# A fused attention and mixture-of-experts block on one core: opening steps in another order, sigmoid by way of silu, halo and logit size on ScalarE, other orders in the steps without a Gram

## The chip, the core and the metric

The kernel runs on one core of a Trainium2 chip. Five engines work side by side, each through its own list of instructions, and meet at semaphores: TensorE (PE in the profile, its weight loads PEld), VectorE (DVE), ScalarE (ACT), GpSimd (POOL), and SyncE (SP), which here only issues DMAs. The metric is the device time of one execution in microseconds; lower is better.

## The reference, cut to what matters

`x` is 8 x 2048 tokens of 256 features, float32.

```python
x = x + attn(layernorm(x));  x = x + ffn(layernorm(x))
# attn: no softmax, one energy matrix per sequence
K, V, Q = x @ wk.T, x @ wv.T, x @ wq.T
energy = einsum('bnd,bne->bde', K, V)                 # 64 x 64 for each of 8 sequences
out = (Q @ energy) * sqrt(3/64) @ wo.T
# ffn
scores = sigmoid(x @ Wr)                              # 8 experts
_, idx = top_k(scores + router_bias, 2)
w = scores[idx];  w = w / (sum(w) + 1e-9);  cw = scatter(w, idx)
hid = silu(x @ Wg[e]) * (x @ Wu[e])                   # e = 0..3, 128 wide
routed = sum_e cw[e] * (hid @ Wd[e]) + (cw[4] + cw[6]) * x + cw[7] * relu(x)
shared = causal depthwise convolution of 4 taps + conv_b
return routed + shared
```

## The kernel before

The 16,384 tokens are 32 groups of 512, four groups to a sequence. A software pipeline of 40 steps works on several groups at once: in step n, group n - LAG[stage] is in that stage (line 34: load -1, norm L 0, Gram A 1, query Q 2, attention B 5, router R 6, experts C 7, output Y 8). Steps 0 to 6 are written out by hand as `head()` on each engine; steps 7 to 39 are `body(st)`. The order of each engine's work is the order of that code; there is no scheduler.

The energy matrix comes from the Gram matrix of the normalised tokens (`gram_halves`, accumulated over four groups in the PSUM bank `ps_gram`). Every fourth step (9, 13, ..., 33) is a chain step: `chain_gramT`, `chain_p1`, `chain_et`, `chain_f` turn a finished Gram into the matrix `f1`/`f2` that `attention` multiplies by the queries. Steps 7 to 32 have a Gram. Step 33 is the last chain step; in steps 34 to 38 `drain()` is true, and 34 to 36 of them still have attention.

Float32 products are made of three or two products of float32r halves: ScalarE copies a PSUM bank to a high half (`xnT_high`, `x2T_out`, `q_high`, `hid_high`), VectorE subtracts it from the bank for the low half (`xnT_low`, `x2T_low`, `q_low`, `hid_low`); for the last expert the subtraction is GpSimd's (`last_low`, L1332).

What happens to one group from attention on, within two steps: VectorE's `residual` adds the attention to the input (L1057) and takes statistics (`norm2_stats`); GpSimd makes scale and shift (`norm_factors`, the shift at L1311); ScalarE normalises four tiles (`norm2`, L840). TensorE transposes them in two halves (`x2_transpose`, L533, into `ps_sh`), multiplies by the router's weights (`router`, L543), and ScalarE copies the logits (`logits_copy`). The sigmoid is 1 / (1 + e^-x): GpSimd's `power` computes e^-x with a pow (L1368, `enx`) and adds one (L1372, `den`); VectorE's `route` takes the reciprocal, adds the bias, finds the two best, and normalises their weights into `cw` (L1115). `weights_transpose` (L606) brings `cw` into rows, ScalarE copies them, SyncE writes them to DRAM and spreads them over the partitions into `cwb`.

The experts, two matrices each (`gate_up(st, k)`, k = 0 to 7, banks k mod 3): ScalarE's silu into `gate` (L763), GpSimd's product with `cwb` (`gate_weight`, L1327), VectorE's product with the other matrix (`hidden`, L1011), the two halves, and `down(st, stage, e)` into `ps_y`. `down` of expert 3 falls in the next step. The convolution runs along the tokens: ScalarE's first tap (`conv_begin`), three on VectorE (`conv_tap`, L1029); three columns of the group before are copied first (`halo`, L1162). VectorE's `output` adds everything up.

## Time and profile before

| What | us |
|---|---|
| Median of 3 runs | 893.69 |
| Lowest and highest | 892.45, 894.4 |
| The profiled execution's own time | 893.6 |
| Its span, first to last instruction | 891.8 |
| TensorE busy | 855.9 |
| VectorE busy | 741.1 |
| ScalarE busy | 628.7 |
| GpSimd busy | 572.7 |

The span is 1.8 us shorter than the execution's own time. Times in the rows count from the span's start. In a timeline row stand start, duration, engine, line, operation, output and inputs by name, shapes and count; brackets at its end give the engine's idle time before it and who ended it. Several equal instructions in a row share one row, with an x and their number. The granted clock of TensorE is given as a share of its full speed, 2.4 GHz.

### The profile page before, as it was taken

Reading aid. Unit: us, or ns where it says so; the run is one execution under the profiler, and the core shown is the slowest. Engines: PE = TensorE matmul, PEld = TensorE weight load, DVE = VectorE, ACT = ScalarE, POOL = GpSimd, SP = SyncE. Lnnn points to the kernel's source line nnn. Section 1 sums busy time; section 2 is a strip of 40 time slices with the busy share of each in tenths; the row PEclk is TensorE's granted clock in tenths of the full one; section 3 lists DMA queues with packets and bytes.
Section 4 is the critical chain, followed back from the end, with each engine's and each line's share of the span. In section 5 each row is a group of like instructions: output and inputs, shape, how many; then the busy total and the mean of one; then the engine's idle time right before and its main releaser. Section 6 shows DMA issues by size and latency. Waiting matters only on the chain.

```text
span 891.8 us, 16729 instructions
## 1 busy us (share of the span) xinstructions
PE 855.9 (96%) x5437; PEld 754.3 (85%) x5437; DVE 741.1 (83%) x2056; ACT 628.7 (71%) x1238; POOL 572.7 (64%) x654
## 2 busy tenths in 40 slices
PE   5789999999999999999999999999999999999997
PEld 4668989898888888988889888888888898788876
DVE  5758889988888998888898888899888887767775
ACT  5676777777687777778677777777777775655643
POOL 3336776667676657667666767666576766556663
PEclk9989999999999999999999999999999999999999
DMA  9111434543334543343544343454424344433333
GB/s 286 57 52 47 137 121 142 143 117 99 95 119 142 144 142 68 114 129 120 143 143 114 101 115 99 143 144 142 119 72 119 101 114 119 111 104 100 106 91 84
DMA packets 79446, 103.86 MB, mean 116 GB/s; under 512 B 6528, under 2 KB 58880, under 8 KB 79360
## 3 DMA queue, kind: packets, MB, share of 16 engines
q1 hardware_dynamic: 74752, 86.02, 30.4%
q0 software_dynamic: 4608, 16.78, 10.0%
q8 instruction: 43, 0.70, 0.3%
q14 instruction: 43, 0.35, 0.1%
HBM read 68.96 MB, written 17.04 MB: 96 GB/s over the span
## 4 chain that ended last, share of the span: by engine, by line
PE 66%; DVE 13%; POOL 12%; issue 5%; ACT 4%; DMA 0%; POOLq 0%; ACTq 0%; DVEq 0%
PE ps_gu L406 9%; PE ps_gu L408 9%; PE ps_gu L407 9%; POOL enx L1368 7%; PE ps_y L406 5%; PE ps_y L408 5%; PE ps_y L407 5%; PE ps_sh L543 4%; PE ps_sh L533 3%; POOL gate L1327 3%; PE ps_sh L516 2%; DVE stats L1065 2%; DVE acc L1057 2%; ACT x L840 2%; PE ps_y L456 2%
## 5 line engine op out<-in xcount | busy, mean ns | idle before, releaser
L1327 POOL TENSOR_TENSOR gate<-gate,cwb 128x512 f32<-128x512 f32 x128 | 167.5, 1309 | 127.8 <-ACT gate L763 126.4
L406 PE MATMUL ps_gu<-x2T_hi,wgu_hi 128*128 128x512 f32 x512 | 212.2, 414 | 0.0
L408 PE MATMUL ps_gu<-x2T_hi,wgu_lo 128*128 128x512 f32 x512 | 203.0, 396 | 0.0
L407 PE MATMUL ps_gu<-x2T_lo,wgu_hi 128*128 128x512 f32 x512 | 202.2, 395 | 0.0
L1368 POOL TENSOR_TENSOR enx<-inv_e,logits 128x32 f32<-128x32 f32 x32 | 177.5, 5546 | 8.6 <-ACT logits L756 8.6
L406 PE MATMUL ps_y<-wd_hi,hid_hi 128*128 128x256 f32 x512 | 152.8, 299 | 4.0 <-DVE hid_lo L1018 3.1
L1029 DVE SCALAR_TENSOR_TENSOR conv<-x2T,conv_w,conv 128x512 f32<-128x512 f32 x192 | 146.4, 801 | 0.0
L408 PE MATMUL ps_y<-wd_hi,hid_lo 128*128 128x256 f32 x512 | 145.3, 284 | 0.0
L407 PE MATMUL ps_y<-wd_lo,hid_hi 128*128 128x256 f32 x512 | 144.2, 282 | 0.0
L1011 DVE TENSOR_TENSOR hid<-ps_gu,gate 128x512 f32<-128x512 f32 x128 | 86.0, 672 | 39.2 <-POOL gate L1327 38.1
L408 PEld LDWEIGHTS ps_gu<-x2T_hi,wgu_lo 128*128 128x128 f32 x512 | 96.9, 189 | 22.5
L406 PEld LDWEIGHTS ps_gu<-x2T_hi,wgu_hi 128*128 128x128 f32 x512 | 97.6, 191 | 19.2 <-DVE hid L1011 3.0
L407 PEld LDWEIGHTS ps_gu<-x2T_lo,wgu_hi 128*128 128x128 f32 x512 | 97.4, 190 | 13.4
L406 PEld LDWEIGHTS ps_y<-wd_hi,hid_hi 128*128 128x128 f32 x512 | 98.5, 192 | 6.7 <-DVE hid_lo L1018 4.3
L763 ACT ACTIVATE gate<-ps_gu 128x512 f32<-128x512 f32 x128 | 75.3, 588 | 40.6 <-PE ps_gu L408 39.0
L1018 DVE TENSOR_TENSOR hid_lo<-hid,hid_hi 128x512 fp32r<-128x512 f32 x96 | 68.8, 716 | 41.6 <-ACT hid_hi L756 41.6
L756 ACT ACTIVATE hid_hi<-hid 128x512 fp32r<-128x512 f32 x128 | 80.2, 626 | 32.1 <-DVE hid L1011 31.5
L407 PEld LDWEIGHTS ps_y<-wd_lo,hid_hi 128*128 128x128 f32 x512 | 97.4, 190 | 1.6
L1306 POOL TENSOR_TENSOR mv<-mv,eps_ln 128x4 f32<-128x4 f32 x64 | 13.5, 211 | 132.2 <-DVE mv L1068 112.8
L408 PEld LDWEIGHTS ps_y<-wd_hi,hid_lo 128*128 128x128 f32 x512 | 97.1, 190 | 0.0
L840 ACT ACTIVATE x<-acc,shift,rstd 128x256 f32<-128x256 f32 x128 | 66.5, 591 | 8.8 <-POOL shift L1311 8.2
L824 ACT ACTIVATE xn<-xa,shift,rstd 128x256 f32<-128x256 f32 x128 | 66.0, 589 | 8.2 <-POOL shift L1311 8.1
(115 smaller groups left out, 1934.3 us busy)
## 6 DMA issues: line engine op xcount, KB each, us to landing
cwb<-cw_rows SPq DMA_DIRECT2D x128, 256.0 KB, 4.0
xa<-in_x SPq DMA_DIRECT2D x32, 512.0 KB, 7.5
acc<-in_x SPq DMA_DIRECT2D x32, 512.0 KB, 6.7
acc<-x POOLq DMA_DIRECT2D x32, 512.0 KB, 4.6
out<-acc SPq DMA_DIRECT2D x64, 256.0 KB, 2.3
cwb<-in_wg SPq DMA_DIRECT2D x4, 128.0 KB, 4.0
cwb<-in_wu SPq DMA_DIRECT2D x4, 128.0 KB, 3.8
cwb<-in_wd SPq DMA_DIRECT2D x1, 512.0 KB, 4.5
```

Source lines behind the costliest of these rows:

```text
L406: nc.tensor.matmul(dst, a_hi, b_hi, start=start, stop=False, skip_group_check=True)
L407: nc.tensor.matmul(dst, a_hi, b_lo, start=False, stop=False, skip_group_check=True)
L408: return nc.tensor.matmul(dst, a_lo, b_hi, start=False, stop=stop, skip_group_check=True)
L756: return nc.scalar.activation(dst, src, ACT.Copy, scale=scale)
L763: nc.scalar.activation(gate[:, e % 2], ps_gu[GU_BANK[2 * e]][:, :], ACT.Silu)\
L824: nc.scalar.activation(xn[:, q, t], xa[:, q, t], ACT.Identity, bias=shift1[:, f, t:t + 1], scale=rstd1[:, f, t:t + 1]).then_inc(xn_ready, 1)
L840: nc.scalar.activation(x2[:, q, t], acc[:, st.slot("B", 4), t], ACT.Identity, bias=shift2[:, q, t:t + 1], scale=rstd2[:, q, t:t + 1]).then ...
L1011: v.tensor_tensor(hid[:, e % 2], ps_gu[GU_BANK[2 * e + 1]][:, :], gate[:, e % 2], ALU.mult)\
L1018: v.tensor_tensor(hid_lo[:, k], hid[:, k], hid_hi[:, k].bitcast(F32), ALU.subtract)\
L1029: v.scalar_tensor_tensor(conv[:, c], x2T[:, q, c, k:k + GT], conv_w[:, c, k:k + 1], conv[:, c], ALU.mult, ALU.add).then_inc(conv_ready, 1)
L1327: g.tensor_tensor(gate[:, e % 2], gate[:, e % 2], cwb[:, q, e], ALU.mult).then_inc(gatew_ready, 1)
L1368: g.tensor_tensor(enx[:, :], inv_e[:, :], logits[:, :], ALU.pow).then_inc(enx_ready, 1)
```

## The change

Four things are changed.

1. The sigmoid. `power` and its two tiles go from GpSimd. ScalarE takes the absolute value of the logits from PSUM (`size`), adds 2^-100 (`mag`, `score_size`) and computes silu(-mag) (`dip`, `score_dip`). VectorE multiplies by the reciprocal of mag, which gives -sigmoid(-|x|), adds 1 where the logit is positive, and takes the absolute value: five operations in front of the bias where there was one. The 1e-9 is a ninth column of `raw`, set once, and its addition (L1106) goes.
2. `halo` moves from VectorE to ScalarE.
3. The opening. The transposes of groups 0 to 4 go to the banks of `ps_y` and `ps_gu` in turn and no longer through `ps_sh`; the chain of the first sequence comes before the first query product's use of the other groups; the first attention is followed by transposes, Gram and query product of the next groups, and only later by the second attention. ScalarE starts with a silu of one element (`spark`), and the program's ScalarE list then has one table load (before: two, the second ahead of the first silu of step 7). In step 7 VectorE takes both `x2T_low` ahead of the convolution's taps.
4. The steps without a Gram. TensorE runs `down(st, "C", 2)` before `weights_transpose` in steps 34 to 36. VectorE runs `residual` and `norm2_stats` ahead of `hid_low(1)`, and `route` is cut in two: `hid_low(2)` stands between its halves in steps 34 to 37. ScalarE runs `hid_high(2)` and then `silu(3)` ahead of `conv_begin`. In step 37 VectorE's `hidden(2)` now stands ahead of the route (before, behind it).

The diff, cut to its core:

```diff
@@ TensorE
             def weights_transpose(st):
                 pe.wait_ge(cw_ready, st.before("R", 1, 1))
...
+            def head_transpose(n):
+                if n >= 2:
+                    pe.wait_ge(xnTlo_ready, (n - 1) * HC)
+                elif n == 1:
+                    pe.wait_ge(wqlo_out, 1)
+                pe.wait_ge(xn_ready, (n + 1) * TG)
+                for c in range(HC):
+                    xn_move(at("A", n, NG), c, head_bank[n][c])
             def head():
...
+                head_transpose(0)
                 pe.wait_ge(w_loaded, 16 * N_LOADS)
                 chain_gramT(b)
                 chain_p1(b)
                 chain_et(b)
+                q_project(at("Q", 0, NG))
                 pe.wait_ge(et_out, b.chains(2, 2))
                 chain_f(b)
+                attention(b, 0)
+                attention(b, 1)
+                head_transpose(1)
+                gram_matrix(at("A", 4, NG))
+                head_transpose(2)
                 q_project(at("Q", 1, NG))
...
                 x2_transpose(r, 0)
                 x2_transpose(r, 1)
+                gram_matrix(at("A", 5, NG))
                 router(r)
+                attention(at("B", 1, NG), 0)
+                attention(at("B", 1, NG), 1)
+                head_transpose(3)
                 q_project(at("Q", 2, NG))
...
                 if a_on:
                     gram_halves(st)
+                if b_on and drain:
+                    down(st, "C", 2)
                 if r_on:
                     weights_transpose(st)
@@ ScalarE
                 copy(logits[:, :], ps_sh[0][:, 0:TG * NE]).then_inc(logits_ready, 1)
+                nc.scalar.activation(size[:, :], ps_sh[0][:, 0:TG * NE], ACT.Abs).then_inc(logits_ready, 1)
...
+                nc.scalar.activation(mag[:, :], size[:, :], ACT.Identity, bias=least[:, :]).then_inc(mag_ready, 1)
+                nc.scalar.activation(dip[:, :], mag[:, :], ACT.Silu, scale=-1.0).then_inc(dip_ready, 1)
...
+                if c_on and st.drain():
+                    hid_high(st, 2)
+                    silu(st, 3)
                 if r_on:
                     conv_begin(st)
-                if c_on:
+                if c_on and not st.drain():
@@ VectorE
-                dve.wait_ge(den_ready, st.before("R", 1, 1))
-                done(v.reciprocal(flat(score[:, :, :]), den[:, :]))
+                dve.wait_ge(mag_ready, st.before("R", 1, 1))
+                done(v.reciprocal(rmag[:, :], mag[:, :]))
+                dve.wait_ge(dip_ready, st.before("R", 1, 1))
+                after()
+                done(v.tensor_tensor(minor[:, :], dip[:, :], rmag[:, :], ALU.mult))
+                after()
+                done(v.scalar_tensor_tensor(signed[:, :], logits[:, :], 0.0, minor[:, :], ALU.is_gt, ALU.add))
+                after()
+                done(v.scalar_tensor_tensor(flat(score[:, :, :]), signed[:, :], -1.0, signed[:, :], ALU.mult, ALU.max))
@@ GpSimd
-                if r_on:
-                    power(st)
```

VectorE in a step without a Gram, from the second `hidden` to the start of the route. Before (L1018 is `hid_low`, L1057 `residual`, L1065 to L1068 the statistics, L1088 the route's start):

```order
L1011 TENSOR_TENSOR hid<-ps_gu,gate 128x512
L1018 TENSOR_TENSOR hid_lo<-hid,hid_hi 128x512
L1057 TENSOR_TENSOR acc<-ps_sh,acc 128x512 x2
L1065 BN_STATS stats<-acc 128x6 x4
L1002 COPY tick<-ident 1x1
L1068 BN_AGGR mv<-stats 128x2 x4
L1011 TENSOR_TENSOR hid<-ps_gu,gate 128x512
L1088 RECIPROCAL score<-den 128x32
L1090 TENSOR_TENSOR biased<-score,bias 128x4x8
```

Now (L1062 is `hid_low`, L1101 `residual`, L1142 to L1157 the route's first half):

```order
L1055 TENSOR_TENSOR hid<-ps_gu,gate 128x512
L1101 TENSOR_TENSOR acc<-ps_sh,acc 128x512 x2
L1109 BN_STATS stats<-acc 128x6 x4
L1046 COPY tick<-ident 1x1
L1112 BN_AGGR mv<-stats 128x2 x4
L1062 TENSOR_TENSOR hid_lo<-hid,hid_hi 128x512
L1055 TENSOR_TENSOR hid<-ps_gu,gate 128x512
L1142 RECIPROCAL rmag<-mag 128x32
L1145 TENSOR_TENSOR minor<-dip,rmag 128x32
L1147 SCALAR_TENSOR_TENSOR signed<-logits,minor 128x32
L1149 SCALAR_TENSOR_TENSOR score<-signed 128x32
L1151 TENSOR_TENSOR biased<-score,bias 128x4x8
```

The residual and its statistics have moved ahead of the first `hid_low`, and the route has grown by three operations here.

TensorE at the end of such a step. Before, from the last product of `gate_up` 7 (L606 is `weights_transpose`):

```order
L408 MATMUL ps_gu<-x2T_hi,wgu_lo 128x512
L606 MATMUL ps_sh<-ident,cw 16x128
L406 MATMUL ps_y<-wd_hi,hid_hi 128x256
L407 MATMUL ps_y<-wd_lo,hid_hi 128x256
L408 MATMUL ps_y<-wd_hi,hid_lo 128x256
```

Now, from the last product of `down` 2 (L600 is `weights_transpose`), with `gate_up` 0 of the next step behind it:

```order
L410 MATMUL ps_y<-wd_hi,hid_hi 128x256
L411 MATMUL ps_y<-wd_lo,hid_hi 128x256
L412 MATMUL ps_y<-wd_hi,hid_lo 128x256
L600 MATMUL ps_sh<-ident,cw 16x128
L410 MATMUL ps_gu<-x2T_hi,wgu_hi 128x512
L411 MATMUL ps_gu<-x2T_lo,wgu_hi 128x512
L412 MATMUL ps_gu<-x2T_hi,wgu_lo 128x512
```

The transposed weights now stand behind the twelve products of `down` 2.

GpSimd in a step with a Gram. Before (L1327 is the gate's product, L1368 the pow):

```order
L1327 TENSOR_TENSOR gate<-gate,cwb 128x512 x2
L1368 TENSOR_TENSOR enx<-inv_e,logits 128x32
L1372 TENSOR_TENSOR den<-enx,one_e 128x32
L1327 TENSOR_TENSOR gate<-gate,cwb 128x512
L1306 TENSOR_TENSOR mv<-mv,eps_ln 128x4
L1307 TENSOR_TENSOR negm<-zero,mv 128x4
L1309 TENSOR_TENSOR rstd<-mv,half_neg 128x4
L1311 TENSOR_TENSOR shift<-negm,rstd 128x4
L1327 TENSOR_TENSOR gate<-gate,cwb 128x512
```

Now (L1387 is the gate's product):

```order
L1387 TENSOR_TENSOR gate<-gate,cwb 128x512 x3
L1366 TENSOR_TENSOR mv<-mv,eps_ln 128x4
L1367 TENSOR_TENSOR negm<-zero,mv 128x4
L1369 TENSOR_TENSOR rstd<-mv,half_neg 128x4
L1371 TENSOR_TENSOR shift<-negm,rstd 128x4
L1387 TENSOR_TENSOR gate<-gate,cwb 128x512
```

The pow and the addition are gone from between the second and the third gate.

VectorE in step 7. Before (L1122 is `x2T_low`, L1029 a tap, L1011 the first `hidden`):

```order
L1183 TENSOR_TENSOR xnT<-ps_sh,xnT 128x512 x2
L1172 COPY x2T<-x2T 128x2x3
L1029 SCALAR_TENSOR_TENSOR conv<-x2T,conv_w,conv 128x512 x2
L1046 BN_STATS stats<-xa 128x6 x4
L1002 COPY tick<-ident 1x1
L1049 BN_AGGR mv<-stats 128x2 x4
L1122 TENSOR_TENSOR x2T_lo<-ps_sh,x2T_hi 128x512
L1029 SCALAR_TENSOR_TENSOR conv<-x2T,conv_w,conv 128x512 x2
L1122 TENSOR_TENSOR x2T_lo<-ps_sh,x2T_hi 128x512
L1011 TENSOR_TENSOR hid<-ps_gu,gate 128x512
```

Now (L1186 is `x2T_low`, L1073 a tap, L1055 the first `hidden`):

```order
L1235 TENSOR_TENSOR xnT<-ps_sh,xnT 128x512 x2
L1186 TENSOR_TENSOR x2T_lo<-ps_sh,x2T_hi 128x512 x2
L1073 SCALAR_TENSOR_TENSOR conv<-x2T,conv_w,conv 128x512 x2
L1090 BN_STATS stats<-xa 128x6 x4
L1046 COPY tick<-ident 1x1
L1093 BN_AGGR mv<-stats 128x2 x4
L1073 SCALAR_TENSOR_TENSOR conv<-x2T,conv_w,conv 128x512 x2
L1055 TENSOR_TENSOR hid<-ps_gu,gate 128x512
```

Both low halves stand ahead of the taps, and the halo's copy is gone.

## Rows read from the trace of the kernel before

**Rows 1.** The page's first table: busy time, share of the span, instructions.
```profile
PE 855.9 (96%) x5437; PEld 754.3 (85%) x5437; DVE 741.1 (83%) x2056; ACT 628.7 (71%) x1238; POOL 572.7 (64%) x654
```

**Rows 2.** Busy time by stretch; last columns PEclk, DMA share, GB/s.
```profile
38.80:59.60 20.80, 17.73 (x84) 15.12 (x85) 10.53 (x41) 14.71 (x28) 7.93 (x10) 0.75 0.00 1
792.00:817.00 25.00, 23.37 (x137) 20.53 (x137) 17.61 (x52) 14.06 (x28) 15.16 (x16) 0.93 0.37 106
817.00:840.50 23.50, 21.86 (x137) 19.18 (x137) 17.62 (x52) 14.06 (x28) 15.16 (x16) 1.00 0.38 113
```

**Rows 3.** Timeline, TensorE: first transposes of x2, and what follows.
```profile
274.79 0.74 PE L533 MATMUL ps_sh<-ident,x 128*128 128x128 f32 x4
275.28 0.36 PE L406 MATMUL ps_y<-wd_hi,hid_hi 128*128 128x256 f32 x1
...
745.01 0.60 PE L533 MATMUL ps_sh<-ident,x 128*128 128x128 f32 x4
745.37 0.37 PE L406 MATMUL ps_y<-wd_hi,hid_hi 128*128 128x256 f32 x1
```

**Rows 4.** Timeline of one step with a Gram, other engines.
```profile
262.79 0.69 DVE L1011 TENSOR_TENSOR hid<-ps_gu,gate 128x512 f32<-128x512 f32 x1 [1.41 <-POOL gate L1327]
265.12 1.29 POOL L1327 TENSOR_TENSOR gate<-gate,cwb 128x512 f32<-128x512 f32 x1 [0.68 <-ACT gate L763]
265.41 1.05 DVE L1101 SCALAR_TENSOR_TENSOR raw<-marked,score 128x32 f32<-128x32 f32 x1
266.72 0.25 DVE L1106 TENSOR_SCALAR wsum_eps<-wsum 128x4 f32<-128x4 f32 x1
272.38 0.59 ACT L756 ACTIVATE xnT<-ps_sh 128x512 fp32r<-128x512 f32 x1
272.83 0.20 POOL L1311 TENSOR_TENSOR shift<-negm,rstd 128x4 f32<-128x4 f32 x1
273.07 2.08 ACT L840 ACTIVATE x<-acc,shift,rstd 128x256 f32<-128x256 f32 x4
```

**Rows 5.** Timeline of one step without a Gram, all engines.
```profile
815.25 1.29 DVE L1106 TENSOR_SCALAR wsum_eps<-wsum 128x4 f32<-128x4 f32 x1
817.05 0.28 PE L606 MATMUL ps_sh<-ident,cw 128*16 128x128 f32 x1 [1.35 <-DVE cw L1115]
817.54 2.06 ACT L840 ACTIVATE x<-acc,shift,rstd 128x256 f32<-128x256 f32 x4
817.63 0.39 PE L406 MATMUL ps_y<-wd_hi,hid_hi 128*128 128x256 f32 x1 [0.30 <-DVE hid_lo L1018]
820.20 1.30 POOL L1332 TENSOR_TENSOR hid_lo<-hid,hid_hi 128x512 fp32r<-128x512 f32 x1 [3.69 <-ACT hid_hi L756]
822.29 0.36 PE L406 MATMUL ps_y<-wd_hi,hid_hi 128*128 128x256 f32 x1
```

**Rows 6.** Timeline: a pow beside a VectorE subtraction, both in SBUF.
```profile
779.28 5.43 POOL L1368 TENSOR_TENSOR enx<-inv_e,logits 128x32 f32<-128x32 f32 x1
783.49 0.69 DVE L1018 TENSOR_TENSOR hid_lo<-hid,hid_hi 128x512 fp32r<-128x512 f32 x1 [1.38 <-ACT hid_hi L756]
```

**Rows 7.** Timeline, TensorE: the last steps.
```profile
862.02 0.28 PE L606 MATMUL ps_sh<-ident,cw 128*16 128x128 f32 x1 [0.30 <-DVE cw L1115]
863.98 0.39 PE L406 MATMUL ps_y<-wd_hi,hid_hi 128*128 128x256 f32 x1 [1.68 <-DVE hid_lo L1018]
883.97 0.38 PE L406 MATMUL ps_y<-wd_hi,hid_hi 128*128 128x256 f32 x1 [0.49 <-DVE hid_lo L1018]
```

**Rows 8.** Timeline: end of the opening and first full step.
```profile
59.63 0.27 PE L606 MATMUL ps_sh<-ident,cw 128*16 128x128 f32 x1
63.52 1.25 PE L533 MATMUL ps_sh<-ident,x 128*128 128x128 f32 x8 [1.82 <-DVE xnT L1183]
70.67 0.68 DVE L1011 TENSOR_TENSOR hid<-ps_gu,gate 128x512 f32<-128x512 f32 x1
72.76 0.42 PE L406 MATMUL ps_gu<-x2T_hi,wgu_hi 128*128 128x512 f32 x1
```

More of the change, by code:

```diff
@@ L744, in body @@
                     xn_transpose(st, 0)
-                if c_on:
+                if c_on and not (b_on and drain):
                     down(st, "C", 2)
@@ L1226, in body @@
                 c_on, y_on, r_on, b_on, m_on = st.on("C"), st.on("Y"), st.on("R"), st.on("B"), st.chain()
-                if r_on:
-                    halo(st)
                 if c_on:
+                    if not st.later("C", 1):
+                        x2T_low(st, 0)
+                        x2T_low(st, 1)
                     dve.wait_ge(halo_ready, st.before("C", 1, 1))
@@ L1233, in body @@
                     norm1_stats(st)
-                if r_on:
+                if r_on and st.later("C", 1):
                     x2T_low(st, 0)
@@ L1251, in body @@
                 drain = st.drain()
+                if b_on and drain:
+                    residual(st, 0)
+                    residual(st, 1)
+                    norm2_stats(st)
                 if c_on:
```

269 lines of the change are left out of this document (134 added, 135 removed).

## The prediction

> **What bounds the kernel now.** I read the table of busy times first: TensorE is busy for 855.9 of 891.8 us [rows 1], so GpSimd's 572.7 us, from which the change takes most, are no bound by themselves. Then I went through the span by stretch and through TensorE's timeline for each idle time and each instruction that takes longer than its like. That gives four places where TensorE loses time.
>
> First, the steps with a Gram. TensorE shows no idle time there, yet the first four transposes of x2 last 0.49 us until the next product begins, where the same four take 0.36 us at 745.01 [rows 3]. I measured this distance for each of the 24 steps between 116 and 720 us: it is always above 0.36, by 0.13 to 0.50 us, and the excess sums to 6.0 us. TensorE waits here, tile by tile, for ScalarE's `norm2`. ScalarE begins it at 273.07, when the shift of GpSimd is there (272.83 + 0.20); ScalarE itself could start some 0.5 us behind the start of its previous copy at 272.38, at 272.88 [rows 4].
>
> Second, the steps without a Gram: TensorE waits 1.35 us for `cw` and 0.30 us for `hid_lo`, three times alike [rows 5]. Third, the granted clock. In two stretches with the same 137 matmul records and the same waits, one has 0.93 of full speed and takes 25.0 us, the other 1.00 and 23.5 us; TensorE's busy time differs by 1.51 us [rows 2]. So a drop to the 1.2 GHz level behind such a wait costs 1.5 us. It came behind one of the three equal waits. Fourth, the opening: TensorE has a granted clock of 0.75 between 38.8 and 59.6 us [rows 2] and waits 1.82 us at 63.52 [rows 8].
>
> The profiled execution took 893.6 us, 1.8 more than its span; the median shown is 893.69, so sums against the one hold for the other.
>
> **Steps with a Gram.** The pow goes, 5.43 us each [rows 6], on an engine that TensorE does not wait for directly. What it frees is the second half of a chain: the third gate's product no longer stands behind it, so `hidden(2)`, which waited 1.41 us for it until 262.79 [rows 4], can start when TensorE has finished `gate_up` 5, by its timeline near 262.3: 0.5 us sooner. The route then gets three operations more, each like the 0.19 us of its small neighbours with some 0.03 between, 0.67 us, and loses L1106 with 0.25 us up to the next one at about 0.29. Net: 0.5 - 0.67 + 0.29, some 0.1 us sooner. But the 1.29 us product of the fourth gate runs from 265.12 to 266.41, and `raw`, which needs about 0.19 us, lasted 1.05 us until 266.46 [rows 4]: it was held up until the product ended. That product starts where TensorE and ScalarE put it, so `raw` ends at 266.46 again, and only the operation behind it is saved: 0.29 us for `cw`, `hid_lo`, the residual and the shift. The shift comes 0.29 us sooner, and then ScalarE's own 272.88 binds: 0.19 us gained. Capped by each step's excess, 24 steps give 4.3 us. Bounds: nothing, if ScalarE's four added small operations (0.2 us each, like its logits copy) hold `norm2` back; 6.0 us, if all excess goes. I take 4.3, since ScalarE waits between 255.5 and 256.4 where the new work stands.
>
> The Trainium skill has a rule on this (SBUF — State Buffer, "Who interferes with whom"): a VectorE instruction with two SBUF inputs contends with a GpSimd instruction that reads SBUF, and the one that comes second blocks until the first is done. For the gate's product the trace agrees (`raw`, 1.05 us). For the pow it does not: a subtraction of two SBUF tiles inside a pow of 5.43 us took 0.69 us [rows 6]. By the rule taking away the pow would free VectorE of blocks as well and the whole excess of 6.0 us would go, a sum of 882.1 us in place of the one below; by the rows it frees nothing there, and I go by them.
>
> **Steps 34 to 36.** Let T be the end of `gate_up` 7. Before, `cw` came at T + 1.35 (in the step shown T is 815.55, read off the timeline), the transposed weights at T + 1.5, and `down` of expert 3 in the next step began at 822.29, T + 6.74 [rows 5]. Now `down` 2 fills T to T + 1.42 (12 products of 0.118), and `weights_transpose` starts at T + 1.45. The residual ahead of `hid_low(1)` brings `cw` to about T + 0.6. TensorE's next 4.3 us of work would put `down` 3 at T + 4.8. But ScalarE's weights copy, `norm2` and `hid_high(3)` and GpSimd's `hid_lo` all hang on `weights_transpose`: `hid_lo` ended 4.45 us behind it (821.50 against 817.05) [rows 5]. That is T + 5.9 now. So the wait is not removed but moved, to 1.2 us ahead of `down` 3, and a step gains 6.74 - 5.97 = 0.77 us; three give 2.3 us. Bounds: 0 and the full 1.65 us a step. The drop of the clock in one of three waits, 1.5 us, comes less often behind waits of 1.2 us: I put two thirds of it, 1.0 us.
>
> **Steps 37 to 39.** Before, the route waited for the pow, and `hidden(2)` for the route; TensorE waited 0.30 and 1.68 us [rows 7], and the clock fell behind it (1.5 us). Now `hidden(2)` runs when `gate_up` 5 is done, and `down` 2 has its input with the transposed weights. The longer route, held up once by the fourth gate's product, puts these at T + 1.05 to 1.75 in place of T + 0.47. `down` 2 then starts 0.7 to 1.3 us sooner; with half of the clock's 1.5 us that is 1.7 us. In the last step `hid_high(2)` ahead of `silu(3)` takes away the 0.49 us wait at 883.97 [rows 7]: 0.5 us. Behind `weights_transpose` hang SyncE's DMAs that spread the weights. For group 31 the first gate's product of step 38 began 7.4 us behind 862.02, of which 0.8 us were ScalarE busy with another copy; 6.6 us behind T + 1.05 to 1.75 it still comes in time for `gate_up` 4, to within 0.2 us. In steps 34 to 36 the DMAs start where they did. Bounds for both terms: 0.4 and 3.3.
>
> **Opening and step 7.** I followed the new order through with the durations of the old one. The Gram of group 3 ends 1 us sooner (no transposes ahead). But the first query product needs the low half of group 0, which VectorE now makes behind the split of the weights, and it stands ahead of `chain_f`: the first attention comes 0.6 us later. From there TensorE has more to do in each wait, and `weights_transpose` comes at about 57.6 instead of 59.63 [rows 8], bound by VectorE's route behind the low halves of group 4. `x2_transpose` comes at 62.1 instead of 63.52. In step 7 VectorE now has both `x2T_low` ahead of its taps and cannot begin them early: from 63.7 it has 5.8 us of work and one block of 1.25 us by a gate's product up to the first `hidden`, 71.1 against 70.67 [rows 8]. TensorE, which was slowed by its clock before and came to `gate_up` 4 at 72.76 [rows 8], gets there at 71.9, but behind a wait of 4 us, after which I expect the low clock, 1.6 us. Net, near 0. Bounds: 2.2 us sooner if the clock stays up and no block falls there; 2 us later if it also falls in the chain of the first sequence, where TensorE waits twice for 2 us. The table load of 1.28 us that goes from step 7 lies beside this wait for VectorE. The halo on ScalarE (0.15 us) lies in its waits for TensorE.
>
> **The sum.** 893.6 - 4.3 - 2.3 - 1.0 - 1.7 - 0.5 - 0 = 883.8 us.
>
> **The rivals.** (1) The opening pays too: the clock stays up through it, 2 to 3 us more, 881.3. For it speaks that TensorE's work is closer together, against it the wait of 4 us in step 7. (2) ScalarE's chain holds `norm2`, so the steps with a Gram give nothing: 893.6 - 5.5 = 888.1. For it: ScalarE's start could be only 0.19 us sooner at best. (3) The drain's wait only moves: clock drops stay, and steps 34 to 39 give 1.5 us in all: 893.6 - 4.3 - 1.5 = 887.8. (4) Both (2) and (3): 892.1, within what can be told from no change. (5) Slower. Place: the route in each step with a Gram. Mechanism: it has more operations with all operands in SBUF (`minor`, `signed`, `score`), and a second one is held up by a gate's product, which costs up to 1.1 us as `raw` does. It decides from the point where the residual starts later than at 267.93, as now; there is no slack, since the transposes wait already. If it is 0.4 us late in 25 steps: + 10 us, less 5.5 of the drain, 898.1. Against it: the third gate's product, the one that could fall on it, now comes 2.5 us before the route.
>
> **How the numbers follow.** Forecast 0.42; (1) 0.16; (2) 0.14; (3) 0.12; (4) 0.07; (5) 0.09. A difference of 0.2%, 1.8 us, is about what a measurement can tell from none. Faster: the forecast, (1), (2) and (3), 0.84; same 0.07; slower 0.09. The range runs from 880.0, all bounds of the drain and the opening together with the 4.3, to 889.5, past (2) and (3).
>
> **What would show it.** Right: the four transposes of x2 at 0.36 to 0.42 us up to the next product in steps with a Gram; a wait of about 1.2 us for GpSimd's `hid_lo` ahead of `down` 3 in steps 35 to 37 and none for `cw` in 34 to 36; `hidden(2)` released by TensorE; a wait of some 4 us for `hid` in step 7. Wrong: steps with a Gram no shorter than 25.4 us, or a new wait for `x` ahead of the transposes; TensorE waiting in the opening more than before; a granted clock below 0.75 there.

## The result, and the profile after

The changed kernel takes 891.18 us (median of 20 runs, 888.78 to 894.38); the kernel before took 895.19 in the runs beside it (892.0 to 901.95). The ratio is 0.9951, 95% interval 0.9936 to 0.9967: faster by 4.4 us, where 9.8 us were forecast, and the time lies above the range (880.0 to 889.5). The profiled run has a span of 888.3 us, 3.5 less than the one before, so the two profiles show most of the difference.

The page's first table of the changed kernel, to be read against [rows 1]:

```profile
PE 849.0 (96%) x5437; PEld 754.3 (85%) x5437; DVE 752.1 (85%) x2088; ACT 643.2 (72%) x1366; POOL 415.6 (47%) x590
```

GpSimd has lost 157 us of work and TensorE, which sets the time, has only 6.9 us less busy time, with 3.4 us more idle time. Where these come from is seen when the span is cut at the transposed weights (L606 before, L600 after), one row for each stretch:

| stretch, from one set of transposed weights to another | before | after | difference | forecast |
|---|---|---|---|---|
| start to step 6 | 59.63 | 59.60 | 0.0 | -2.0 |
| step 7 | 26.23 | 30.05 | +3.8 | +2.0 |
| 25 steps, nearly all with a Gram (85.86 to 739.84; 89.65 to 739.33) | 653.98 | 649.68 | -4.3 | -4.3 |
| the rest, to TensorE's last product | 148.4 | 145.5 | -3.0 | -5.5 |

(The forecast put the opening and step 7 at 0 together; -2.0 is its transposed weights at 57.6.) So one term came out as worked, one that was put at 0 cost 3.8 us, and one is too small. In this table, and wherever a length of "step 7" is given, a step ends with its transposed weights.

**Steps with a Gram.** The timeline of the changed kernel in the step that answers to [rows 3, 4], 3.04 us later in the span by TensorE's transposes of x2 (3.05 by the fourth gate's product):

```profile
268.17 1.30 POOL L1387 TENSOR_TENSOR gate<-gate,cwb 128x512 f32<-128x512 f32 x1 [1.85 <-ACT gate L765]
268.76 0.75 DVE L1167 SCALAR_TENSOR_TENSOR raw<-marked,score 128x32 f32<-128x32 f32 x1
275.60 0.20 POOL L1371 TENSOR_TENSOR shift<-negm,rstd 128x4 f32<-128x4 f32 x1
275.89 2.07 ACT L842 ACTIVATE x<-acc,shift,rstd 128x256 f32<-128x256 f32 x4
277.83 0.60 PE L531 MATMUL ps_sh<-ident,x 128*128 128x128 f32 x4
278.19 0.36 PE L410 MATMUL ps_y<-wd_hi,hid_hi 128*128 128x256 f32 x1
```

`raw` ends at 269.51, less the 3.04 at 266.47, as before (266.46): the fourth gate's product still holds it. The shift comes at 272.56 (0.27 sooner), `norm2` at 272.85 (0.22 sooner), and the four transposes last 0.36 us up to the next product where they took 0.49. Seven steps in 25, six of them behind a chain, keep 0.52 to 0.70 us; the others are at 0.35 or 0.36.

**Step 7.** TensorE and VectorE from step 6 to `gate_up` 4, to be read against [rows 8]:

```profile
59.60 0.28 PE L600 MATMUL ps_sh<-ident,cw 128*16 128x128 f32 x1 [2.04 <-DVE cw L1179]
64.13 1.25 PE L531 MATMUL ps_sh<-ident,x 128*128 128x128 f32 x8 [1.82 <-DVE xnT L1235]
65.94 0.69 DVE L1186 TENSOR_TENSOR x2T_lo<-ps_sh,x2T_hi 128x512 fp32r<-128x512 f32 x1 [1.27 <-ACT x2T_hi L758]
67.53 2.50 DVE L1073 SCALAR_TENSOR_TENSOR conv<-x2T,conv_w,conv 128x512 f32<-128x512 f32 x2
73.03 0.67 DVE L1055 TENSOR_TENSOR hid<-ps_gu,gate 128x512 f32<-128x512 f32 x1
73.76 0.79 PE L410 MATMUL ps_gu<-x2T_hi,wgu_hi 128*128 128x512 f32 x1 [3.57 <-DVE hid L1055]
```

The wait of some 4 us is there (3.57), but all of it is 2 us later than worked out: the transposes of x2 at 64.13 and not 62.1, `hidden` at 73.03 and not 71.1, since TensorE waits 2.04 us for `cw` in step 6 (L600 at 59.60). The same stretch in the view by stretch, before first, then the changed kernel, then experiment e10 (below), in which no wait of step 7 is longer than 1.82 us. The last columns are PEclk (the granted clock), DMA share and GB/s:

```profile
59.60:85.80 26.20, 22.58 (x134) 19.48 (x133) 20.48 (x54) 18.07 (x34) 14.98 (x11) 0.93 0.26 76
```
```profile
59.60:89.60 30.00, 24.21 (x133) 20.58 (x134) 21.75 (x57) 17.45 (x37) 9.78 (x13) 0.89 0.25 67
```
```profile
57.80:82.00 24.20, 21.50 (x133) 18.27 (x134) 20.82 (x56) 18.57 (x39) 9.81 (x13) 1.00 0.29 80
```

TensorE's work takes 21.5 us at the 2.4 GHz level (e10, granted clock 1.00); the falls to the 1.2 GHz level cost 1.1 us before (22.58) and 2.7 us after (24.21), where the clock was 0.50 from 73.8 to 79.5, behind the wait of 3.57 us. The 3.8 us are then 2.2 of idle time (5.8 less 3.6) and 1.6 of clock.

**The last steps.** TensorE's waits in the changed kernel, against [rows 5, 7], and the pow of `norm2` of step 33 with what VectorE does beside it (the last two rows):

```profile
773.11 0.73 PE L531 MATMUL ps_sh<-ident,x 128*128 128x128 f32 x2 [2.15 <-ACT x L842]
816.16 0.28 PE L600 MATMUL ps_sh<-ident,cw 128*16 128x128 f32 x1 [0.21 <-DVE cw L1179]
820.63 0.39 PE L410 MATMUL ps_y<-wd_hi,hid_hi 128*128 128x256 f32 x1 [0.94 <-POOL hid_lo L1392]
861.51 0.28 PE L600 MATMUL ps_sh<-ident,cw 128*16 128x128 f32 x1 [1.87 <-DVE cw L1179]
872.15 1.09 PE L460 MATMUL ps_y<-ident,conv 128*128 128x128 f32 x8 [0.45 <-DVE conv L1073]
883.10 0.39 PE L410 MATMUL ps_y<-wd_hi,hid_hi 128*128 128x256 f32 x1 [1.41 <-POOL hid_lo L1392]
769.26 2.79 POOL L1369 TENSOR_TENSOR rstd<-mv,half_neg 128x4 f32<-128x4 f32 x1
769.75 1.39 DVE L1073 SCALAR_TENSOR_TENSOR conv<-x2T,conv_w,conv 128x512 f32<-128x512 f32 x2
```

The same place before:

```profile
769.46 0.67 DVE L1135 TENSOR_TENSOR q<-ps_gu,q 64x512 fp32r<-64x512 f32 x1
769.56 1.49 POOL L1309 TENSOR_TENSOR rstd<-mv,half_neg 128x4 f32<-128x4 f32 x1
770.07 0.73 DVE L1029 SCALAR_TENSOR_TENSOR conv<-x2T,conv_w,conv 128x512 f32<-128x512 f32 x1
770.08 0.06 DVE L1170 MEMSET x2T<- 128x6 f32 x1
770.73 0.73 DVE L1029 SCALAR_TENSOR_TENSOR conv<-x2T,conv_w,conv 128x512 f32<-128x512 f32 x1
```

From the transposed weights of step 33 TensorE is idle for 9.8 us before and 10.0 us after. The waits at the transposed weights of steps 34 to 36 and behind them are 1.14 us each in place of 1.64. But the stretch from the transposed weights of step 33 to those of step 34 (766.30 to 793.11 in the changed kernel; it is called step 33 from here on) has 2.8 us in place of 1.4, and the rest has 0.3 us more. What is gained here is granted clock: TensorE's busy time from 766 us on is 3.0 us shorter, 111.8 before and 108.8 after, with two drops before (0.93 in 792 to 817, 0.62 in 864 to 867) and none in this run of the changed kernel:

```profile
793.10:861.50 68.40, 63.33 (x391) 55.52 (x391) 54.59 (x146) 43.64 (x96) 27.15 (x38) 1.00 0.38 109
```

### The profile page after: what moved, and what is told of

Its sections match the earlier page's. It is cut to its first block, busy times and chain, and to the rows that moved or that the text cites. A ratio compares the mean times of both kernels' runs of the same rounds, so it can differ in the third digit from the quotient of the medians.

```text
span 888.3 us, 16852 instructions
## 1 busy us (share of the span) xinstructions
PE 849.0 (96%) x5437; PEld 754.3 (85%) x5437; DVE 752.1 (85%) x2088; ACT 643.2 (72%) x1366; POOL 415.6 (47%) x590
## 4 chain that ended last, share of the span: by engine, by line
PE 77%; DVE 9%; ACT 4%; issue 4%; POOL 4%; DMA 1%; POOLq 0%; DVEq 0%; ACTq 0%
PE ps_gu L410 11%; PE ps_gu L412 10%; PE ps_gu L411 10%; PE ps_sh L541 6%; PE ps_y L410 5%; PE ps_y L411 5%; PE ps_y L412 5%; PE ps_sh L531 3%; PE ps_y L460 3%; PE ps_sh L484 2%; POOL rstd L1369 1%; PE ps_gram L476 1%; PE ps_gu L564 1%; PE ps_sh L588 1%; PE ps_gram L618 1%
## 5 line engine op out<-in xcount | busy, mean ns | idle before, releaser
L1387 POOL TENSOR_TENSOR gate<-gate,cwb 128x512 f32<-128x512 f32 x128 | 165.7, 1294 | 277.4 <-ACT gate L765 269.3
L1073 DVE SCALAR_TENSOR_TENSOR conv<-x2T,conv_w,conv 128x512 f32<-128x512 f32 x192 | 153.6, 838 | 0.0
L1062 DVE TENSOR_TENSOR hid_lo<-hid,hid_hi 128x512 fp32r<-128x512 f32 x96 | 83.2, 866 | 38.1 <-ACT hid_hi L758 38.1
L1055 DVE TENSOR_TENSOR hid<-ps_gu,gate 128x512 f32<-128x512 f32 x128 | 86.2, 673 | 20.0 <-issue 13.4
L1366 POOL TENSOR_TENSOR mv<-mv,eps_ln 128x4 f32<-128x4 f32 x64 | 24.9, 388 | 136.6 <-DVE mv L1112 114.6
L1369 POOL TENSOR_TENSOR rstd<-mv,half_neg 128x4 f32<-128x4 f32 x64 | 67.2, 1050 | 5.0
```

The lines of the kernel that those rows point to most:

```text
L1055: v.tensor_tensor(hid[:, e % 2], ps_gu[GU_BANK[2 * e + 1]][:, :], gate[:, e % 2], ALU.mult)\
L1062: v.tensor_tensor(hid_lo[:, k], hid[:, k], hid_hi[:, k].bitcast(F32), ALU.subtract)\
L1073: v.scalar_tensor_tensor(conv[:, c], x2T[:, q, c, k:k + GT], conv_w[:, c, k:k + 1], conv[:, c], ALU.mult, ALU.add).then_inc(conv_ready, 1)
L1369: g.tensor_tensor(rstd, mv[:, :, 1], half_neg[:, :], ALU.pow).then_inc(rstd_ready, 1)
L1387: g.tensor_tensor(gate[:, e % 2], gate[:, e % 2], cwb[:, q, e], ALU.mult).then_inc(gatew_ready, 1)
```

## The experiments

Each is compared with the kernel before on the same chip; "span" is that of its one profiled run. Runs of one kernel differ by 1 to 10 us in this program (the kernel before: 892.0 to 901.95). Much of that goes with the clock: of the 11 runs of the kernel before that stand beside e9, the slowest, 901.13 us, has a mean granted clock of 0.979 and the fastest, 891.49, one of 0.992. So a mechanism is read in the trace from the stretch it sits in, and its worth from the ratio.

### e1: the opening of before in the changed kernel

All four `head()` functions and the waits and banks that go with them are as before; `spark`, `score_size`, `score_dip` and `halo` stay on ScalarE. In VectorE's `body`, step 7 has the order of before; the edit's first lines:

```diff
-                    if not st.later("C", 1):
-                        x2T_low(st, 0)
-                        x2T_low(st, 1)
...
```


> The changed kernel with the opening of the kernel before (all engines, with its banks and its order of VectorE in step 7; halo on ScalarE and the sigmoid from silu stay). Theory: the new opening and step 7 alone lose 3.8 us (the transposed weights of step 7, 89.65 against 85.86), and the Gram steps (-4.1) and the last steps (-3.0) keep theirs: span 884.5, some 3.8 us under the changed kernel, the transposed weights of step 7 at about 85.9. Rival: the gain of the Gram steps was there only because the changed opening leaves the engines in another phase; then those steps take 25.3 to 25.4 us each again and the span is about 888.

Measured: 889.56 us, ratio 0.9951 (0.9937 to 0.9966), span 887.3. Step 7 takes 26.19 us, as before (26.23), and the Gram steps keep their gain (649.8 us). But the transposed weights of step 6 came at 61.70 and not near 59.6, since the clock fell in the first chain (before, it was 1.00 in the same 8 us); the span missed the 884.5 expected by 2.8 us, 2.1 of them here:

```profile
30.00:38.00 8.00, 7.29 (x29) 5.76 (x28) 6.53 (x21) 4.27 (x10) 3.05 (x8) 0.57 0.00 1
```

So the rival is out, and the theory holds for step 7. The ratio is that of the changed kernel: what the new opening with its step 7 costs in the profile can't be told from such a drop (2 us), which comes in either order (0.50 in the changed kernel's 30 to 38 us).

### e2: the first taps of a step without Q behind the pow

```diff
+                    if not st.on("Q"):
+                        dve.wait_ge(rstd2_ready, st.before("B"))
                     conv_tap(st, 0)
```


> The changed kernel, with VectorE's first taps of each step that has no Q waiting for the pow of norm2 of the step before. Theory: the pow that takes 2.79 us at 769.26 (1.03 elsewhere) is held up by the two taps that VectorE runs beside it from 769.75 to 771.14; with the taps behind it, it takes 1.03 us, norm2 begins 1.7 us sooner, TensorE's wait of 2.15 us ahead of the transposes of x2 shrinks to about 0.4, and the span is 886.6. Rival: the pow is long for another reason (its operands, the DMA beside it): still near 2.8 us, TensorE waits as before or longer by the taps, 888.3 to 889.

Measured: 890.59 us, ratio 0.9966 (0.9954 to 0.9978), span 889.3. Step 33 takes 25.05 us in place of 26.81, and the pow is as short as elsewhere:

```profile
771.34 1.03 POOL L1371 TENSOR_TENSOR rstd<-mv,half_neg 128x4 f32<-128x4 f32 x1
773.43 0.73 PE L531 MATMUL ps_sh<-ident,x 128*128 128x128 f32 x2 [0.41 <-ACT x L842]
```

The theory holds to 0.1 us. The span, 886.6 expected, hides it: in this run the transposed weights of step 7 came 2 us later than in the changed kernel's (91.63), and the clock fell behind the wait of 1.87 us in step 37. The ratio shows no gain over the changed kernel's 0.9951.

### e3: another order on VectorE in step 7

```diff
+                seven = c_on and not st.later("C", 1)
                 if c_on:
-                    if not st.later("C", 1):
-                        x2T_low(st, 0)
-                        x2T_low(st, 1)
                     dve.wait_ge(halo_ready, st.before("C", 1, 1))
                     conv_tap(st, 0)
-                if st.on("L"):
+                    if seven:
+                        x2T_low(st, 0)
+                        x2T_low(st, 1)
+                if st.on("L") and not seven:
                     norm1_stats(st)
...
                     hidden(st, 1)
+                if seven:
+                    norm1_stats(st)
```


> The changed kernel, in step 7 alone with another order on VectorE: first taps, both low halves of x2, second taps, hidden 0, and the norm1 statistics (1.9 us) only behind hidden 1. Theory: TensorE's wait of 3.57 us for hidden 0 at 73.76 and the low clock behind it (to 79.5) come from the order on VectorE: hidden 0 starts at about 70 instead of 73.03, the wait shrinks to under 1 us, the clock stays up, the transposed weights of step 7 come at 84 to 86 instead of 89.65, span 882.5 to 885. Rival: VectorE has as much to do in step 7 either way, so the wait moves to the next product that needs a later hidden, and the statistics come late for norm1: at most 1 us gained, 887.5.

Measured: 889.95 us, ratio 0.996 (0.9946 to 0.9975), span 884.4, the transposed weights of step 7 at 85.53 (expected 84 to 86; 89.65 in the changed kernel):

```profile
64.41 2.45 DVE L1073 SCALAR_TENSOR_TENSOR conv<-x2T,conv_w,conv 128x512 f32<-128x512 f32 x2
66.78 1.27 DVE L1186 TENSOR_TENSOR x2T_lo<-ps_sh,x2T_hi 128x512 fp32r<-128x512 f32 x2
69.78 0.68 DVE L1055 TENSOR_TENSOR hid<-ps_gu,gate 128x512 f32<-128x512 f32 x1
67.61 2.22 PE L541 MATMUL ps_sh<-wr_sb,x2T 128*128 128x8 f32 x16 [1.00 <-DVE x2T_lo L1186]
```

The taps fill the time in which VectorE waited for ScalarE, `hidden` starts at 69.78, and of the wait of 3.57 us a wait of 1.00 us for the router is left. The clock fell all the same (0.52 in 69.7 to 72.6). The profiled run was the fastest of seven (886.21, their median 889.95), so the span flatters the edit: its ratio is no better than the changed kernel's.

### e4: VectorE's split of the weights later

```diff
-                split_weights()
...
                 f_low(b)
+                split_weights(0, 1)
...
                 xnT_low_head(1, 1)
+                split_weights(1, 2)
```


> The changed kernel, in the opening with VectorE's three low halves of the weights (3.5 us) behind the transposes of group 0 and the first F, in place of ahead of them. Theory: TensorE's wait of 2.10 us ahead of the first query product (29.31) goes, and with it the granted clock of 0.50 that holds from there to 38.7; the first attention begins at about 31 instead of 33.83, transposed weights of step 6 at 57 or sooner instead of 59.60, span some 2 us shorter, 886. Rival: the clock falls at the other waits of the first chain (0.37 us twice, 1.33 us) whatever the order, and what is gained is lost again at the wait for route: no gain, 888.3.

Measured: 890.86 us, ratio 0.9955 (0.9935 to 0.9975), span 890.0. The first chain ran at full clock, but the transposed weights of step 6 came at 59.91: TensorE waited 1.86 us for `norm2` at 40.63 and the route was no sooner. Of the rival, the first half fell (the clock stayed up) and the second holds: the gain is lost again ahead of the route, which hangs on something else.

```profile
30.00:38.00 8.00, 6.08 (x43) 5.53 (x43) 7.11 (x17) 6.36 (x14) 2.98 (x8) 1.00 0.01 2
```

### e5: the old order of step 7 alone

```diff
-                    if not st.later("C", 1):
-                        x2T_low(st, 0)
-                        x2T_low(st, 1)
...
-                if r_on and st.later("C", 1):
+                if r_on:
                     x2T_low(st, 0)
```


> The changed kernel, with VectorE's order in step 7 as before (first taps, norm1 statistics, low half 0 of x2, second taps, low half 1, hidden 0); the opening stays new. Theory: of the 3.8 us lost up to the transposed weights of step 7, most come from this order, which keeps VectorE idle until 65.94 and hidden 0 back to 73.03. With the old order hidden 0 comes at about 71.5 and TensorE's idle time is split in two (ahead of the router and ahead of gate_up 4), the step from 59.6 takes 26 to 27.5 us instead of 30.05: span 885 to 886. Rival: the loss comes from the opening steps (route and transposes of x2 in step 7 later by 0.6 us), the step takes 29 us or more: 887.5 to 888.3.

Measured: 892.31 us, ratio 0.9953 (0.9934 to 0.9973), span 890.8. The step takes 29.34 us: my expectation of 26 to 27.5 was wrong and the rival right. The taps come first, but a gate's product of GpSimd (64.83 to 66.36) falls on them and they last 2.45 us where they took 1.41 before, so the router waits 2.76 us for the low half:

```profile
64.46 2.45 DVE L1073 SCALAR_TENSOR_TENSOR conv<-x2T,conv_w,conv 128x512 f32<-128x512 f32 x2
64.83 1.53 POOL L1384 TENSOR_TENSOR gate<-gate,cwb 128x512 f32<-128x512 f32 x1 [4.54 <-DMA cwb<-cw_rows]
```

With the old opening ahead of it (e1) the old order took 26.19 us.

### e6: the old orders in the steps without a Gram

```diff
-                if b_on and drain:
-                    down(st, "C", 2)
                 if r_on:
                     weights_transpose(st)
...
-                if c_on and st.drain():
-                    hid_high(st, 2)
-                    silu(st, 3)
```

VectorE's order is `hid_low` 1, residual, `norm2_stats`, `hidden` 2, the route in one piece, `hid_low` 2 (in step 37 the route ahead of `hidden` 2), as before.

> The changed kernel with the orders of the kernel before in the steps without a Gram (TensorE's down 2 behind the transposed weights; VectorE's residual behind hid_low 1 and the route in one piece; ScalarE's hid_high 2 behind silu 3). Theory: TensorE's idle time in steps 33 to 39 is 10.0 us in the changed kernel and 9.8 in the one before, so the new orders moved waits and took none away; what the profile after has less (3.0 us) are two drops of the granted clock. Then the old orders give the same span but for drops: from the transposed weights of step 32 to the end 149.0 (no drop) to 152.0 us (two drops), time within 0.2% of the changed kernel or up to 1.5 us slower. Rival: the new orders are worth the idle time of steps 34 to 36 (0.5 us each) and more: 2.5 us slower in every execution.

Measured: 896.36 us, ratio 1.0001 (0.998 to 1.0021), span 893.7: the new orders are worth as much as the whole change, whose gain is gone without them, though the 25 steps keep theirs (649.8 us). My theory, that these orders were worth nothing, falls. TensorE waits 2.92 us in each of steps 34 to 36, not 1.64 as before:

```profile
816.08 1.27 POOL L1380 TENSOR_TENSOR gate<-gate,cwb 128x512 f32<-128x512 f32 x1
816.11 1.25 DVE L1152 COPY two<-top 128x8 f32<-128x8 f32 x1
819.08 0.28 PE L600 MATMUL ps_sh<-ident,cw 128*16 128x128 f32 x1 [2.62 <-DVE cw L1174]
```

The route, longer by three operations (four stand ahead of the bias where one stood, not five as the description of the change has it), stands behind the residual; one of its operations is held for 1.25 us by the fourth gate's product (before it was `wsum_eps`, 1.29 us [rows 5]), and more of the route comes after it. From step 33 on TensorE is idle for 13.7 us, 3.7 more than with the new orders; the pow of step 33 takes 2.79 us here too.

### e7: one small operation put back into the route

```diff
-                done(v.reciprocal(winv[:, :], wsum[:, :]))
+                done(v.tensor_scalar(wsum_eps[:, :], wsum[:, :], 0.0, None, ALU.add))
+                after()
+                done(v.reciprocal(winv[:, :], wsum_eps[:, :]))
```


> The changed kernel with one more small operation on VectorE in the route, behind the sum of the weights (where the kernel before added its epsilon; here it adds 0). Theory: in the Gram steps the end of the fourth gate's product sets raw, and what stands behind raw sets the shift: cw comes 0.25 to 0.29 us later, the first transposes of x2 last 0.49 to 0.58 us again in three of four steps, these 24 steps give back nearly all of their 4.1 us: span 892. Rival: the gain of these steps comes from the pow's absence (hidden 2 no longer waits, no contention), then they keep at least 3 of the 4.1 us: span 888 to 889.

Measured: 897.52 us, ratio 1.0013 (0.9996 to 1.003), span 891.5 (the profiled run, 893.3, was the fastest of twelve). The 25 steps take 654.2 us, 4.6 more than in the changed kernel and 0.3 more than before; the first transposes of x2 are at 0.50 to 0.64 us in most, at 0.85 or 0.86 behind a chain. In the step of [rows 4]:

```profile
269.11 0.25 DVE L1173 TENSOR_SCALAR wsum_eps<-wsum 128x4 f32<-128x4 f32 x1
277.11 0.82 PE L532 MATMUL ps_sh<-ident,x 128*128 128x128 f32 x4
277.69 0.36 PE L411 MATMUL ps_y<-wd_hi,hid_hi 128*128 128x256 f32 x1
```

The theory holds: the gain of the Gram steps hangs on one operation of 0.25 us behind `raw`. That the pow is gone (5.43 us) and the route has three operations more ahead of `raw` leaves nothing there to see; no run has the one without the other, so what each is worth alone is not shown.

### e8: e2 and e3 together

The edits are those two, unchanged.

> The two edits together that each shortened its stretch: VectorE's order in step 7 (first taps, low halves, second taps, hidden 0, statistics behind hidden 1) and its first taps behind the pow of norm2 in the steps with no Q. Theory: they are independent (3.95 us in step 7, 1.76 us in step 33): span 882.6, time some 4 to 6 us under the changed kernel on the same chip, if the clock falls as often. Rival: less idle time in one place brings the drop of the clock to another, as it seems for each edit alone (medians only 0.6 and 1.2 us under the changed kernel): within 2 us of it.

Measured: 885.97 us (883.5 to 888.96), ratio 0.9885 (0.9858 to 0.9912), span 884.4. Step 33 takes 25.06 us; step 7 takes 28.32 with only 2.4 us of idle time in it, since the clock was at 0.50 from 65.2 to 75.4 us of this run. Together they are worth more than the two ratios alone (0.9966, 0.996) let one expect; why is not shown.

### e9: last steps, `hid_high` 3 ahead of `norm2`; VectorE makes the last low half

```diff
                 if st.on("B") and st.drain():
+                    hid_high(st, 3)
                     norm2(st)
...
-                if c_on:
+                if c_on and not (st.on("B") and st.drain()):
                     hid_high(st, 3)
...
                     hidden(st, 3)
+                    if st.before("C") == NG - 1:
+                        hid_low(st, 3)
...
-                if c_on:
+                if c_on and st.before("C") != NG - 1:
                     last_low(st)
```


> The fastest kernel so far (step 7's order on VectorE and the taps behind the pow), with two edits in the last steps: where there is no Gram, ScalarE makes hid_high 3 ahead of norm2 instead of behind it, and in the last step VectorE (0.69 us) makes the low half of expert 3's hidden instead of GpSimd (1.26 us). Theory: TensorE's wait of 0.93 us for hid_lo ahead of down 3 comes from the 2.07 us of norm2 in front of hid_high 3; in its place at most 0.3 us for x are left, three times; the last wait of 1.41 us becomes 0.84. From the transposed weights of step 33 to the end 2.2 to 2.6 us less idle time than 8.3 us. Rival: norm2, now 0.5 us later, holds up the transposes of x2, and the wait only changes its name: under 0.8 us gained.

Measured on e8: 881.72 us (879.89 to 885.42), ratio 0.9854 (0.9819 to 0.9888), span 879.2. From step 33 on 5.0 us of idle time, where e8 has 8.3: more than expected, because no wait for `x` takes the place of the one removed.

```profile
810.31 0.63 ACT L758 ACTIVATE hid_hi<-hid 128x512 fp32r<-128x512 f32 x1
810.84 2.06 ACT L842 ACTIVATE x<-acc,shift,rstd 128x256 f32<-128x256 f32 x4
873.99 0.39 PE L410 MATMUL ps_y<-wd_hi,hid_hi 128*128 128x256 f32 x1 [0.80 <-DVE hid_lo L1063]
```

### e10: opening, the copies of group 4 ahead of `norm1` of group 6

```diff
-                norm1(at("L", 6, NG))
                 xnT_head(4, 0)
                 xnT_head(4, 1)
+                norm1(at("L", 6, NG))
```


> The fastest kernel so far, with one edit in the opening: ScalarE copies the transposes of group 4 ahead of norm1 of group 6 (2.08 us), not behind it. Theory: TensorE's wait of 2.04 us for the weights of group 0 ahead of the transposed weights of step 6 comes from the route, which stands on VectorE behind the low halves of group 4, and these behind ScalarE's copies; the route starts 1.2 us sooner (then VectorE's own work ahead of it binds), the wait shrinks to about 0.85 us and the transposed weights of step 6 come at 57.9 in place of 59.09. Rival: the third query product or norm2 of group 1 comes late instead, and the transposed weights stay at 59 or later.

Measured on e8: 881.62 us (880.89 to 881.89), ratio 0.9849 (0.9817 to 0.988), span 879.1. In the changed kernel (first two rows) and in e10 (the others):

```profile
52.12 2.08 ACT L826 ACTIVATE xn<-xa,shift,rstd 128x256 f32<-128x256 f32 x4
54.10 1.06 ACT L758 ACTIVATE xnT<-ps_y 128x512 fp32r<-128x512 f32 x2
```
```profile
51.55 1.09 ACT L758 ACTIVATE xnT<-ps_y 128x512 fp32r<-128x512 f32 x2
52.52 2.07 ACT L826 ACTIVATE xn<-xa,shift,rstd 128x256 f32<-128x256 f32 x4
57.77 0.28 PE L600 MATMUL ps_sh<-ident,cw 128*16 128x128 f32 x1 [0.75 <-DVE cw L1179]
68.82 0.50 PE L410 MATMUL ps_gu<-x2T_hi,wgu_hi 128*128 128x512 f32 x1 [0.47 <-DVE hid L1055]
```

The transposed weights of step 6 come at 57.77, where e8, which differs in this block alone, has them at 59.09 with the same wait of 2.04 us as the changed kernel. The first chain ran at a clock of 0.51 here too (30 to 38 us): this block, and not the clock, made the route 1.3 us late.

### e11 and e12: both edits, and the later split on top

e11 has the edits of e9 and e10, e12 that of e4 as well.

> Both of these edits on the fastest kernel so far. Theory: they add up, 3.4 to 3.8 us less than the 884.4 us of its profiled run: span about 881, time about 8 us less than the changed kernel. Rival: drops of the clock (1.5 us each, at different waits in each run) hide it: no more than 1.5 us under the fastest so far.

> The same with VectorE's low halves of the weights (3.5 us) taken behind the transposes of group 0, as tried before on the changed kernel. Theory: there it took the wait of 2.10 us ahead of the first query product away and the first chain ran at full clock, but the gain was lost again at the wait for norm2 (1.86 us at 40.63) and at the route; with norm1 of group 6 out of ScalarE's way the route is no longer late, and the transposed weights of step 6 come at 56 to 57. Rival: what ScalarE does between 34 and 40 us binds the opening whatever stands around it: no sooner than without this edit.

Measured: e11 879.9 us (878.64 to 880.76), ratio 0.983 (0.9795 to 0.9865), span 877.0; e12 878.83 us (876.4 to 881.39), ratio 0.9817 (0.9782 to 0.9851), span 878.1. e11's span is 7.4 us under e8's, but not as the sum of the two edits: step 7 is 3.8 us shorter, since the clock did not fall there in this run (24.5 us at 1.00), the last steps 3.8 us, and the opening is 0.3 us longer. The wait for `cw` in step 6 is 0.75 us as in e10, yet the transposed weights come at 59.41, for the whole opening of this run is 1.6 us later than e10's (the query product ahead of the experts at 54.74, there 53.10). By the medians e11 is 1.7 to 1.8 us below e9 and e10, and the three intervals overlap. In e12 the transposed weights of step 6 come at 57.40, sooner than e10's but not at 56 to 57, and the clock was at the 1.2 GHz level from 62.9 to 73.0 us of step 7; whether the later split is worth anything is open, the intervals overlap. Either beats both kernels clearly: 1.2 to 1.3% under the changed kernel, by its ratio of 0.9951.

## Why the prediction was wrong, and where it was right

**Steps with a Gram, -4.3 forecast, -4.3 measured: right by its mechanism, its size in part by luck.** The product holds `raw` (266.46 and 266.47), only the operation behind it is saved (0.27 against 0.29), `norm2` moves by 0.22 (0.19). e7 undoes it with that one operation. The rival that ScalarE holds `norm2` (2) and the slower one (5) are both out. The trace also bears out that the pow did not hinder VectorE here, against what the Trainium skill would give (SBUF — State Buffer, "Who interferes with whom"): the 6.0 us by the rule did not come. The even share was wrong, though. I capped every step's gain at 0.19 us; the six steps behind a chain gained nothing (25.43 us before and 25.46 after at the last of them), and the other steps from step 9 on gained 0.11 to 0.57 us each. The sum of the two errors is near zero.

**Opening and step 7, 0 forecast, +3.8 measured: the term that failed most.** Its step that `weights_transpose` comes at about 57.6, "bound by VectorE's route behind the low halves of group 4", is where it broke: it came at 59.60, behind a wait of 2.04 us for `cw`. I took VectorE's own queue as the bound and left out that these low halves need ScalarE's copies, which stand behind a `norm1` of 2.08 us; the route, now behind the low halves, inherits that. e10 moves this one block: against e8 the wait shrinks from 2.04 to 0.75 us and the transposed weights come 1.3 us sooner, at 57.77. The other half microsecond is not this block: the query product ahead of the experts came at 53.65 in the changed kernel's run and at 53.10 and 53.13 in e10's and e8's. The step for `hidden` in step 7 had the right work (5.8 us and a block of 1.25; measured 7.09 from 65.94 to 73.03) but started it 2.2 us too soon, at 63.7; from there its own terms give 70.75 and not the 71.1 of the text. The low clock, forecast at 1.6 us behind the wait, cost 2.7 in the whole step. The price I named as the bound for this (2 us later "if it also falls in the chain") was met in size by another cause: the clock did fall in that chain (0.50 in 30 to 38 us), but so it did in e10, and e4, where it did not, came to 59.91. It was also one of the signs named for being wrong, with TensorE waiting more in the opening: in the first 59.6 us it is busy for 40.55 us, before for 42.07.

**Steps 33 to 39, -5.5 forecast, -3.0 measured.** Four terms. (a) Steps 34 to 36: the wait for `cw` did move to `hid_lo` ahead of `down` 3 (0.94, forecast 1.2), but 0.21 us for `cw` stays, and a step has 0.50 us less idle time, not 0.77: -1.5 in place of -2.3. (b) Steps 37 to 39: nothing. The waits of 0.30 us for `cw` and 1.68 us for `hid_lo` became one of 1.87 us for `cw`, above the 1.05 to 1.75 forecast for the longer route; the 0.49 us at the end went into the 0.93 behind it (1.41), and 0.45 for the taps was new: +0.3 in all, in place of -1.45 (the two terms without their 0.75 of clock). (c) Step 33, which the prediction did not look at: +1.4, of which 1.1 is the wait behind the pow that the taps hold up (2.15 us, before 1.06) and 0.3 a wait for the residual ahead of the transposed weights of step 33. The pow takes 2.79 us in place of 1.49. e2 puts the taps behind it and has 1.03; so the taps hold it. Why they hold it for 1.3 us longer than before is not shown: in both kernels they start 0.5 us behind it and run back to back. What is gone from VectorE just there is the halo's MEMSET ahead of the taps, now on ScalarE, and every kernel of this document with the halo on ScalarE and no gate for the taps has the 2.79 us (e1, e3 to e7), but no run moves the halo alone. (d) The clock gave 3.0 and not 1.75, in these two profiles; over runs it cannot be told from these medians. And the terms did not stand alone: by e6 the longer route with the old orders waits 2.92 us in each of steps 34 to 36 where 1.64 stood before, 3.8 us in all, and the new orders first have to win that back. I had counted the new operations in the Gram steps and left them out in steps 34 to 36.

The lower end of the range, 880.0, was said to be all bounds of the drain and the opening with the 4.3 us. By the bounds as named (4.95 and 3.3 us for the drain, 2.2 for the opening, 1.0 of clock) it would be about 877.9. The result lies at the other end, so nothing hangs on it.

What stays open: what decides behind which wait the clock falls. The same wait of 1.82 us for the transposes of x2 in step 7 passed without a fall in e10 and with one in e8 (from 65.2 us on), and the 1.87 us for `cw` in step 37 without one in the changed kernel and with one in e2 (863.1 to 866.4).

## What to carry to other kernels

When an instruction is moved on one engine, follow its inputs on the others to the instruction that stands in front of them in the new order: a block of 2 us on ScalarE set a route on VectorE that looked bound by VectorE. A big operation taken off an engine that is not waited for need not show in the time: here the steps with a Gram gained by one operation of 0.25 us behind the one that is held, 4.3 us over 25 steps. What replaces it must be priced again in each kind of step. And in a kernel whose clock falls behind waits, it can pay to take the waits away in several places before judging by the time: two edits that alone had ratios (0.9966 and 0.996) no better than the changed kernel's 0.9951 had 0.9885 together.

## What the runs showed of the hardware

A GpSimd pow on 128x4 elements takes 1.01 to 1.04 us in 63 of the changed kernel's 64, and 2.79 us in the one that VectorE's taps run beside; with the taps behind it, 1.03. It had begun 0.49 us ahead of them, so here it was the first of the two that was held, where the Trainium skill (SBUF — State Buffer, "Who interferes with whom") lets the second one wait. In the kernel before, with the same taps beside it, it takes 1.49 us. In e9 two such pows take 1.51 and 1.52 us; they start 0.07 and 0.06 us behind VectorE's `hid_lo`, which has both inputs in SBUF and takes 0.68 us. The same pair of taps takes 1.4 us without a gate's product beside it and 2.45 us (e5) and 2.50 us (changed kernel) with one.

Some small VectorE operations that start beside a gate's product end with it: `raw`, `wsum_eps` and the copy of `two` (1.05, 1.29 and 1.25 us; `raw` takes 0.19 us in six steps of the kernel before). Not all do. In the changed kernel MATCH_REPLACE8 starts inside such a product and takes its usual 0.14 us, and `raw` right behind it is held to the product's end (815.37):

```profile
814.08 1.29 POOL L1387 TENSOR_TENSOR gate<-gate,cwb 128x512 f32<-128x512 f32 x1
814.11 0.14 DVE L1165 MATCH_REPLACE8 marked<-two,biased 128x14 f32<-128x14 f32 x1
814.28 1.13 DVE L1167 SCALAR_TENSOR_TENSOR raw<-marked,score 128x32 f32<-128x32 f32 x1
```
